# A linear-attention layer, an attention layer and two expert layers on one core: every item of a step placed by a table

## The reference

```python
x = x + 0.5 * ffn0(layernorm(x))        # int8-like weights CB, scale SCB, bias
x = x + deltanet(layernorm(x))          # the linear layer, below
x = x + 0.5 * ffn0(layernorm(x))
x = x + 0.5 * moe(layernorm(x))         # 16-head softmax attention, then 4 experts of 128-512-128
x = x + proj_ln_attn(layernorm(x))      # q, k, v each projected and layer-normed, one head
x = x + 0.5 * moe(layernorm(x))

def deltanet(x):                        # 8 heads of 16, J = 2 decays per head
    q, k = elu(x @ Wq.T) + 1, elu(x @ Wk.T) + 1
    v, beta, mix = x @ Wv.T, x @ Wbeta.T + bbeta, x @ Wmix.T + bmix
    gate = sigmoid(x @ Wgate.T + bgate)
    for t in range(256):                # carried state S (16x16) and z (16) per head and decay
        S = S * min(sigmoid(beta[t]) * r, 0.9999) + gate[t] * outer(k[t], v[t])
        z = z * min(sigmoid(beta[t]) * r, 0.9999) + gate[t] * k[t]
        y[t] = sum_j softmax(mix[t]) * (q[t] @ S) / (q[t] @ z + 1e-6)
    h = x + y @ Wout.T + bout
    return layernorm(h) * ln_g + ln_b
```

## Time and profile before

| | |
|---|---|
| median of 3 runs | 1615.6 us (1615.12 to 1621.57) |
| the profiled execution's own time | 1624.56 us |
| its span, first to last instruction | 1622.4 us |
| busy: PE, DVE, ACT, POOL | 74%, 58%, 51%, 42% |
| mean granted TensorE clock | 0.836 |
| largest wait in section 5 of the page | DVE's reduction L2075, 192.9 us idle before it |

### The profile page before, as it was taken

How to read it: one execution, slowest core, us unless ns; L and a number is a source line. 1 busy time by engine, 2 the same in 40 slices (tenths; PEclk the granted TensorE clock), 3 DMA queues, 4 the chain that set the end, 5 groups by cost and what they waited for, 6 DMA issues and landing times.

```text
span 1622.4 us, 30206 instructions
## 1 busy us (share of the span) xinstructions
PE 1193.1 (74%) x10624; PEld 774.4 (48%) x10624; DVE 942.2 (58%) x2992; ACT 822.2 (51%) x1849; POOL 688.0 (42%) x679
## 2 busy tenths in 40 slices
PE   3688888887446678988997567556667899899753
PEld 3566666655312335645555346333232565555543
DVE  5345556546336577677753696644667777775221
ACT  3444445443413557767775224232355777766532
POOL 4323333334622133555444566652213356544442
PEclk9878889888556789899999788866687999999977
DMA  7000000000022234443422120002223444442232
GB/s 240 1 2 1 1 2 2 1 1 2 2 78 80 80 98 135 129 143 117 125 76 77 45 63 24 12 1 78 80 80 98 139 133 147 133 134 73 64 106 71
DMA packets 116338, 116.71 MB, mean 72 GB/s; under 512 B 9288, under 2 KB 100040, under 8 KB 116040
## 3 DMA queue, kind: packets, MB, share of 16 engines
q1 hardware_dynamic: 105184, 77.99, 15.5%
q0 software_dynamic: 11008, 36.81, 7.0%
HBM read 73.01 MB, written 42.15 MB: 71 GB/s over the span
## 4 chain that ended last, share of the span: by engine, by line
PE 49%; DVE 14%; issue 8%; POOL 8%; ACT 8%; DMA 7%; SPq 5%; POOLq 0%; ACTq 0%; DVEq 0%
PE bank L1477 6%; PE bank L1514 6%; PE bank L1491 6%; PE bank L1535 5%; SPq L697 3%; DMA scr_m<-MH 2%; PE bank L1252 2%; DVE NM L2075 2%; PE bank L1310 2%; PE bank L1717 2%; PE bank L1553 2%; POOL scr_x L839 2%; POOL YG L847 1%; PE bank L1281 1%; SPq L662 1%
## 5 line engine op out<-in xcount | busy, mean ns | idle before, releaser
L2075 DVE TENSOR_REDUCE NM<-bank 128x2 f32<-128x512 f32 x512 | 338.0, 684 | 192.9 <-PE bank L1541 189.5
L1100 ACT ACTIVATE PBS<-bank 128x512 f32<-128x512 f32 x512 | 299.5, 600 | 219.5 <-PE bank L1535 216.1
L1535 PE MATMUL bank<-QS,KS 50*128 50x256 bf16 x1024 | 197.9, 295 | 100.2 <-DMA QS<-scr_m 49.4
L740 POOL TENSOR_TENSOR rs<-ve,half 128x4 f32<-128x4 f32 x88 | 89.9, 1022 | 421.2 <-DVE ve L1986 281.5
L1541 PE MATMUL bank<-KS,QS 48*128 48x256 bf16 x1024 | 208.5, 305 | 37.7 <-DMA KS<-scr_k 25.3
L1535 PEld LDWEIGHTS bank<-QS,KS 50*128 50x128 bf16 x1024 | 64.1, 97 | 231.5 <-issue 114.2
L1514 PE MATMUL bank<-PBS,V 128*32 128x256 f32 x2048 | 156.8, 429 | 1.4 <-ACT PBS L1100 1.4
L839 POOL DMA_INDIRECT scr_x<-XS,POS x64 | 63.8, 996 | 98.5 <-DVE POS L2041 83.9
L972 ACT ACTIVATE DB<-bank 128x512 f32<-128x512 f32 x64 | 38.5, 602 | 130.9 <-PE bank L1266 130.8
L1541 PEld LDWEIGHTS bank<-KS,QS 48*128 48x128 bf16 x1024 | 63.8, 98 | 66.4 <-DVE NM L2075 38.1
L1802 DVE TENSOR_TENSOR AB<-DB,bank 128x512 f32<-128x512 f32 x64 | 43.9, 685 | 81.7 <-ACT DB L972 47.7
(11 more groups left out here) (308 smaller groups left out, 2744.5 us busy)
## 6 DMA issues: line engine op xcount, KB each, us to landing
QS<-scr_q SPq DMA_DIRECT2D x64, 192.0 KB
KS<-scr_k SPq DMA_DIRECT2D x64, 192.0 KB
XD<-scr_x SPq DMA_DIRECT2D x16, 448.0 KB
scr_q<-PQ SPq DMA_DIRECT2D x32, 192.0 KB, 2.1
scr_k<-PQ SPq DMA_DIRECT2D x32, 192.0 KB, 2.2
scr_q<-PQ SPq DMA_DIRECT2D x32, 128.0 KB, 2.1
scr_k<-PQ SPq DMA_DIRECT2D x32, 128.0 KB, 2.1
scr_y<-YB SPq DMA_DIRECT2D x16, 256.0 KB, 2.3
```

Of the source, the lines that this page charges most:

```text
L740: pool.tensor_tensor(rs_[:, :], ve_[:, :], half[:, 0:ve_.shape[1]], ALU.pow).then_inc(rstd_sem, 1)
L1100: act.activation(PB[i % PB_SLOTS][:, :, :], bank[1 + i % 2][:, :].rearrange("p (k t) -> p k t", k=2), ACT.Exp).then_inc(A.e, 1)
L1535: last_s = pe.matmul(bank[1 + s % 2][:, k * T:(k + 1) * T], KS[1 - par][r, b, s // 2, k * P:(k + 1) * P], QS[1 - par][r, b, s // 2, :], st ...
L2075: dve.tensor_reduce(NM[:, 2 * b + qt, h:h + 3:2], bank[3 + i % 2][:, :].rearrange("p (u t) -> p u t", u=2), AX_X, ALU.max, negate=True).th ...
```

## The change

The linear layer's step becomes a loop over 16 slots, and a table LT gives every item of every engine its slot; ORDER is now sorted from it. AT, TAIL and ATTN have new numbers. LEADS is written with FFN_AT. No item is added, left out or changed in what it computes. One wait of POOL's YR asks for all earlier uses of bank 7 where it asked for those up to t1. The first part of the diff:

```diff
--- before.py
+++ after.py
@@ -46,24 +46,24 @@
 WROW = B2_AT + P
 
 
-AT = {"x_stats": 0, "x_moments": 0, "max1": 3, "div2": 6, "div3": 7, "z": 12, "z_stats": 13, "z_moments": 13, "q_mid":
-      11, "k_mid": 15, "acc": 14, "acc_stats": 17, "acc_moments": 17, "max0": 17, "take0": 24, "div0": 21, "div1": 24,
-      "x_add": 29, "take1": 30, "key": (21, 24, 25, 27, 28), "place": (30, 31, 31, 33), "m1T": 0, "turn2": 6, "turn3":
-      8, "x_turn": 7, "q": 9, "anT": 9, "k": 11, "wo": 12, "v": 13, "xd0": 14, "xd1": 14, "up": (15, 17, 19, 21, 23,
-      25, 27), "down": (18, 20, 21, 24, 27, 28, 30), "m0T": 17, "turn0": 19, "turn1": 24, "ranks": 30, "y": (4, 5),
-      "yt": 7, "qev": 9, "kev": 12, "anc": 9, "vev": 12, "zn": (17, 18), "en": (21, 22), "xt0": 13, "xt1": 14, "relu":
-      (15, 17, 19, 21, 23, 25, 27), "x_rstd": 0, "scatter": 2, "gather": 2, "v1": 4, "weights": 7, "rest1": (6, 14),
-      "z_rstd": 14, "rest2": (16, 17), "acc_rstd": 19, "xs": 20, "eg": 20, "yr": 28}
-
-
-TAIL = {"x_stats": 0, "x_moments": 0, "max1": 9, "div2": 6, "div3": 7, "z": 12, "z_stats": 13, "z_moments": 13, "q_mid":
-        13, "k_mid": 15, "acc": 11, "acc_stats": 16, "acc_moments": 19, "max0": 17, "take0": 24, "div0": 19, "div1": 24,
-        "x_add": 29, "take1": 30, "key": (21, 24, 25, 28, 28), "place": (30, 31, 31, 33), "m1T": 1, "turn2": 5, "turn3":
-        7, "x_turn": 7, "q": 6, "anT": 9, "k": 14, "wo": 12, "v": 13, "xd0": 14, "xd1": 15, "up": (15, 17, 19, 21, 23,
-        25, 27), "down": (18, 20, 21, 24, 27, 28, 30), "m0T": 18, "turn0": 21, "turn1": 24, "ranks": 30, "y": (4, 5),
-        "yt": 8, "qev": 9, "kev": 12, "anc": 9, "vev": 14, "zn": (17, 18), "en": (21, 22), "xt0": 13, "xt1": 15, "relu":
-        (15, 17, 19, 21, 23, 25, 27), "x_rstd": 4, "scatter": 0, "gather": 4, "v1": 4, "weights": 5, "rest1": (11, 14),
-        "z_rstd": 14, "rest2": (16, 17), "acc_rstd": 16, "xs": 20, "eg": 20, "yr": 29}
+AT = {"x_stats": 0, "x_moments": 0, "max1": 3, "div2": 6, "div3": 8, "z": 12, "z_stats": 13, "z_moments": 13, "q_mid":
+      12, "k_mid": 15, "acc": 15, "acc_stats": 17, "acc_moments": 17, "max0": 17, "take0": 23, "div0": 22, "div1": 28,
+      "x_add": 28, "take1": 30, "key": (21, 24, 26, 28, 28), "place": (31, 31, 31, 33), "m1T": 2, "turn2": 4, "turn3":
+      8, "x_turn": 7, "q": 9, "anT": 9, "k": 11, "wo": 12, "v": 13, "xd0": 14, "xd1": 15, "up": (15, 17, 19, 21, 23,
+      25, 27), "down": (18, 19, 21, 24, 27, 28, 30), "m0T": 16, "turn0": 19, "turn1": 24, "ranks": 30, "y": (4, 5),
+      "yt": 7, "qev": 9, "kev": 12, "anc": 9, "vev": 12, "zn": (17, 18), "en": (20, 23), "xt0": 13, "xt1": 15, "relu":
+      (15, 17, 19, 21, 23, 25, 27), "x_rstd": 0, "scatter": 3, "gather": 3, "v1": 4, "weights": 6, "rest1": (4, 14),
+      "z_rstd": 14, "rest2": (16, 16), "acc_rstd": 17, "xs": 17, "eg": 24, "yr": 29}
+
+
+TAIL = {"x_stats": 0, "x_moments": 0, "max1": 4, "div2": 5, "div3": 7, "z": 12, "z_stats": 12, "z_moments": 15, "q_mid":
+        12, "k_mid": 13, "acc": 13, "acc_stats": 16, "acc_moments": 17, "max0": 17, "take0": 27, "div0": 20, "div1": 29,
+        "x_add": 28, "take1": 30, "key": (17, 17, 20, 25, 25), "place": (31, 31, 31, 34), "m1T": 0, "turn2": 2, "turn3":
+        7, "x_turn": 9, "q": 9, "anT": 7, "k": 12, "wo": 15, "v": 9, "xd0": 15, "xd1": 15, "up": (15, 17, 19, 21, 23,
+        25, 27), "down": (18, 20, 21, 24, 27, 28, 30), "m0T": 15, "turn0": 20, "turn1": 23, "ranks": 30, "y": (5, 6),
+        "yt": 8, "qev": 3, "kev": 10, "anc": 10, "vev": 19, "zn": (17, 18), "en": (21, 23), "xt0": 14, "xt1": 15,
+        "relu": (15, 17, 19, 21, 23, 25, 27), "x_rstd": 1, "scatter": 2, "gather": 2, "v1": 0, "weights": 5, "rest1":
+        (11, 15), "z_rstd": 11, "rest2": (18, 22), "acc_rstd": 16, "xs": 24, "eg": 25, "yr": 30}
 
 
 def placed(slot):
@@ -73,30 +73,43 @@
 
 ATTN = {
     33: ((0, "pre"),),
-    39: ((0, "scale"), (0, "turn"), (0, "raw")),
+    39: ((0, "turn"), (0, "scale")),
+    41: ((0, "raw"),),
     44: ((1, "pre"),),
-    47: ((0, "norm"), (1, "scale"), (0, "yx"), (1, "turn"), (1, "raw"), (0, "kq")),
+    47: ((1, "scale"), (0, "norm"), (0, "yx"), (1, "turn"), (0, "kq"), (1, "raw")),
+    57: ((1, "yx"),),
     58: ((2, "pre"),),
-    61: ((2, "scale"), (1, "norm"), (1, "yx"), (0, "max"), (2, "turn"), (2, "raw"), (0, "exp"), (0, "main"), (3,
-        "pre")),
-    68: ((1, "kq"),),
+    60: ((2, "scale"),),
+    61: ((1, "norm"), (0, "max"), (2, "raw"), (2, "turn"), (0, "exp"), (0, "main"), (3, "pre")),
+    63: ((1, "kq"),),
+    68: ((2, "yx"),),
+    69: ((2, "norm"),),
     70: ((3, "scale"),),
-    71: ((2, "yx"), (2, "norm"), (1, "max"), (3, "turn"), (1, "exp"), (3, "raw"), (1, "main"), (2, "kq")),
-    76: ((4, "pre"),),
-    78: ((4, "scale"),),
+    71: ((1, "max"),),
+    72: ((1, "exp"),),
+    74: ((3, "turn"),),
+    75: ((3, "raw"), (1, "main")),
+    76: ((4, "pre"), (2, "kq")),
+    77: ((4, "scale"),),
     79: ((3, "norm"), (2, "max"), (4, "turn"), (2, "exp"), (4, "raw"), (2, "main")),
     80: ((3, "yx"),),
+    82: ((3, "kq"),),
     87: ((5, "pre"),),
-    90: ((5, "scale"), (3, "kq")),
-    93: ((4, "norm"), (3, "max"), (4, "yx"), (5, "turn"), (3, "exp"), (5, "raw"), (3, "main"), (5, "yx")),
+    89: ((5, "scale"),),
+    93: ((4, "yx"), (4, "norm"), (3, "max"), (5, "turn"), (5, "raw"), (3, "exp"), (5, "yx")),
+    102: ((3, "main"),),
     104: ((4, "kq"),),
-    106: ((6, "pre"),),
-    107: ((6, "scale"), (5, "norm"), (4, "max"), (6, "turn"), (4, "exp"), (6, "raw"), (4, "main"), (5, "kq")),
-    128: ((7, "pre"),),
-    130: ((7, "scale"), (6, "norm")),
-    131: ((6, "yx"), (5, "max"), (7, "turn"), (5, "exp"), (7, "raw"), (5, "main"), (6, "kq")),
-    132: ((7, "norm"), (6, "max"), (7, "yx"), (6, "exp"), (6, "main"), (7, "kq")),
-    133: ((7, "max"), (7, "exp"), (7, "main")),
+    105: ((6, "pre"),),
+    106: ((6, "scale"),),
+    107: ((5, "norm"), (4, "max"), (6, "turn"), (4, "exp"), (6, "raw"), (4, "main")),
+    109: ((5, "kq"),),
+    124: ((6, "yx"),),
+    125: ((7, "pre"),),
+    128: ((7, "scale"),),
+    130: ((6, "norm"),),
+    131: ((5, "max"), (7, "turn"), (5, "exp"), (7, "raw")),
+    132: ((5, "main"), (6, "kq"), (7, "norm"), (6, "max"), (6, "exp"), (6, "main")),
+    133: ((7, "kq"), (7, "max"), (7, "yx"), (7, "exp"), (7, "main")),
 }
 EXPERTS_AT = 133
 
@@ -115,12 +128,33 @@
 PACKED = _at
 
 
-ORDER = {1: (("yt", "pre"), ("mg", "pre"), ("cb0", "main"), ("q", "pre"), ("cb1", "main"), ("k", "pre"),
-             ("lw", "pre"), ("nst", "pre"), ("stk", "pre")),
-         6: (("t0", "post"), ("t2", "post"), ("v", "pre"), ("yo", "post"), ("s0", "main"), ("s2", "main"),
-             ("s4", "main")),
-         7: (("t1", "post"), ("t3", "post"), ("kt", "main"), ("wo", "post"), ("s1", "main"), ("s3", "main"),
-             ("s5", "main"))}
+FFN_AT = (0, 2, 4, 7, 8, 10, 12)
+LSLOTS = 16
+LT = {"weigh": (1, 3, 4, 6, 8, 10, 12, 13), "decay": (0, 2, 4, 6, 8, 10, 12, 13), "grow": (1, 2, 4, 6, 8, 10, 12, 14),
+      "yt": 0, "mg": 1, "cb": (4, 6), "scores1": 5, "nst": 11, "sums": (4, 7, 12, 1), "t": (2, 2, 4, 4), "kt": 9, "v":
+      7, "qk": (4, 6), "lw": 7, "yo": 8, "wo": 10, "s": (10, 12, 12, 14, 14, 15), "stk": 13, "scores0": 14, "a_yt": 0,
+      "a_ln": 4, "copy": (8, 1), "a_e1": 2, "a_cb": (3, 5), "a_qk": (4, 6), "a_kt": 9, "a_qx": 6, "a_we": 7, "a_yo":
+      8, "a_nst": 13, "a_stk": 13, "a_hn": 15, "a_x": 14, "vw": (0, 5), "qp": (1, 6), "yr": 4, "x_rstd": 6, "h_rstd":
+      12, "hg": 15, "d_mg": 1, "d_t": (3, 6), "d_sd": 3, "d_qf": 7, "d_lb": 3, "d_kf": 11, "d_gate": 6, "d_v": 8,
+      "x_stats": 7, "d_bt": 9, "x_moments": 10, "d_h": 12, "h_moments": 12, "d_s": (12, 12, 12, 14, 14, 14)}
+
+
+def order(b):
+
+    one = {1: (("yt", "pre"), ("mg", "pre"), ("cb0", "main"), ("cb1", "main"), ("nst", "pre"), ("q", "pre"), ("k", "pre"),
+               ("lw", "pre"), ("stk", "pre")),
+           6: (("t0", "post"), ("t2", "post"), ("v", "pre"), ("yo", "post"), ("s0", "main"), ("s2", "main"), ("s4", "main")),
+           7: (("t1", "post"), ("t3", "post"), ("kt", "main"), ("wo", "post"), ("s1", "main"), ("s3", "main"),
+               ("s5", "main"))}[b]
+
+    def slot(name):
+        if name in LT:
+            return LT[name]
+        return LT["qk"]["qk".index(name)] if name in "qk" else LT[name[:-1]][int(name[-1])]
+    return tuple(sorted(one, key=lambda use: slot(use[0])))
+
+
+ORDER = {b: order(b) for b in (1, 6, 7)}
 
 
 def uses(b, n, on, name=None):
```

In the loops each fixed number gives way to its entry of LT, as here on PE (the items stand in this order within a slot):

```diff
                                                  start=True, stop=True)
                         last.then_inc(L.full[1], 1)
 
-                    for i in range(8):
-                        if pre and i == 0:
+                    for i in range(LSLOTS):
+                        if pre and i == LT["yt"]:
                             pe.wait_ge(L.norm, n + 2)
                             turn(1, "yt", lambda t: Y0[other][:, t, :])
-                        if post and i == 0:
```

(52 more changed lines are left out.)

153 lines of the change are left out of this document (80 added, 73 removed).

## The result

The changed kernel takes **1527.63 us** (median of 4 runs, 1522.95 to 1530.24) against 1615.36 us before it on the same chip: a ratio of 0.9444 (95% interval 0.9411 to 0.9477), 88 us less. The forecast was 1585, with 1563 as the lower end. The sign was right and the size was not. The profiled execution took 1526.71 us (span 1524.9), 97.5 us less span than the profiled one before.

A forecast was written before the change was run, and what follows sets the result against it. No engine's total was taken to bound the kernel (PE busiest, 74%), so only PE's waits could go. Linear layer -23, AT -3 and tail -5 gave -31 us, 1615.6 to 1584.6, said as 1585; range 1576 to 1595, with neighbours 1563 to 1607.

The forecast's parts named there:

- The linear layer's order, 3.5 us a step of waits: Linear steps: reordering removes PE waits, walked as 3.9 us a step, taken as 3.5; -23 us in all.
- cb1's 1.2: Linear step: cb1's wait for q's two evacuations, 1.2 us, goes because scores1 now stands between.
- wo's 0.8: Linear step: wo's 1.9 us wait for yo's copy falls to about 1.1, gain 0.8.
- k's: Linear step: k's 1.7 us wait for cb1's copy shrinks as Ln and its loads run before q; gain 1.6.
- yo, which I had gain 0.6: Linear step: yo's 0.6 us wait for v's evacuation on DVE goes, since lw and d5 follow v.
- the states': Linear step: the states' 1.0 us wait for DVE's masking shrinks, gain 0.8.
- STK's: Linear step: new wait of d0' behind stk for ACT's copy, loss 0.6; a 0.5 us wait was to show.
- rival 2: Gains compound: linear steps' clock rises from 0.87 to 0.95, worth 1.9 us a step, giving 1572; chance 0.15.
- AT, -3: Expert layers' table: new order gains 3 us in all, from +5 to -12.
- m1T's wait of 1.0: Expert steps: m1T in slot 2 removes PE's 1.0 us wait for the last reduction, merely moved to slot 1's.
- The tail, -5 by scale(1): First expert tail: scale(1) before norm(0) avoids some 7 us of DVE contention with POOL; -5, from +8 to -12.
- The second tail, 0: Second expert layer's tail: z goes ahead of acc, but the chain keeps its order; 0 us, from +3 to -3.

The follow-up runs named there:

- scores1_back: Changed kernel with PE's scores1 alone put back behind k, ACT's Ln staying ahead of q's evacuation: 1528.53 us, ratio 0.9431.
- kt_back: Changed kernel with kt on PE put back ahead of v: 1533.70 us, ratio 0.9436.
- lin_alone: Changed kernel with the old AT, TAIL and ATTN, so only the linear layer's table is new: 1561.61 us, ratio 0.9623.
- norm_first: Changed kernel with norm(0) put back ahead of scale(1) on DVE, in ATTN: 1536.42 us, ratio 0.9492.
- tail_alone: Kernel before with only the new TAIL and ATTN: 1611.32 us, ratio 0.9938.
- at_alone: Kernel before with only the new AT: 1598.93 us, ratio 0.9884.
- fill_new: Changed kernel with the score matmuls of slot 2 issued six times over in every expert step: 1537.94 us, ratio 0.9474.
- fill_full: Changed kernel with the repeated score matmuls of slot 2 in expert steps 4 to 7 of each layer alone: 1532.35 us, ratio 0.9444.

## Why the prediction was right or wrong

- **The linear layer's order, 3.5 us a step of waits: nearly right in sum.** PE's idle time in the five full steps was 200.1 less 165.8 of busy time, 6.9 us a step, and is 2.9 now (160.8 less 146.5, over five). That is 4.0 gained, against a walk of 3.9. The sum came out partly by luck, as its terms show.
- **Its terms: wrong.** I added five waits as if each had its own worth. cb1's 1.2 and wo's 0.8 are worth 0.5 and 0.2 of idle time by themselves (scores1_back, kt_back), since yo's wait behind them takes up the rest; k's was worth 2.1 of idle time, not 1.6, and scores1 another 1.0 with Ln late. yo, which I had gain 0.6, lost 0.8. wo's wait fell by 1.5, not by 0.8, and the states' by 0.7 of the 0.8. The 0.5 us of new wait for Ln did not come, and STK's came with 0.5.
- **The step that failed first: the clock, put at nothing in the sum.** I priced the linear steps by idle time alone. The same matmuls of a step take 3.9 us less, from 33.2 to 29.3 us busy, as the clock goes from 0.87 to 0.98. That is as much again as the waits, and the direction of rival 2. It had a chance of 0.15 and a price of 1.9 us a step for 0.08 of clock. By its own slope, 2.8 us for 0.12, a rise of 0.11 gives 2.6; measured 3.9. With its price rival 2 would have said 1572, 44 us above the measured time.
- **Which steps count: wrong.** I gave 4.5 us to the steps up to the first X and 1 to the two behind the full ones. They gave 10 to 11, and 13.8 (34.5 and 36.2 us, now 24.4 and 32.5). Some 3 us of the 13.8 are matmuls that now lie ahead of the first X, so the gain ahead of it is larger by as much. Where the rest went was not tried.
- **AT, -3: wrong, it is about -19, give or take 10.** m1T's wait of 1.0 went, as said. Full steps idle 4.1 to 4.3 us, but for one, where lin_alone's idle 4.6 and the kernel before idles 4.5 to 5.5. Wrong was to price the order by idle time alone: PE's busy time fell by 1.5 us a step against the kernel before and by 3.0 against the step of lin_alone, as the half level got shorter. Why it got shorter stays open.
- **The tail, -5 by scale(1): near in number by luck, wrong in reason.** Profiles give -4.0 for this pair and about -9 over all kernels. The contention that the 5 us were reckoned from is worth 0, and its 8.54 us were misread as the length of two POOL products, which is 6.95. I had counted kq(0)'s later start, but took only 3.6 of the 8 us for it, where it took all.
- **The second tail, 0: within its range**, 184.0 and 181.9 us.
- **What was to show it.** The waits for CB and for re gone, STK at 0.5, scale(1) at 1.1: as said. The wait at L1296 gone: no, it grew to 1.3. The one at L1372 about 1: 0.4. Steps of 35 to 37 us: 32.2 on average. The wait at L1592 gone: yes, but the one for the reduction grew by 0.75 a step only against lin_alone (5.4 and 6.9 in two steps); against the kernel before it did not in the second layer (7.1). No 15 us before turn(1): 6.75.

The forecast fell 57 us short. Some 19 of them are the clock in the five full linear steps (3.9 each), some 19 the linear layer's steps around them (10 to 11 and 13.8, where 5.5 were said), which no run takes apart, some 16 AT and some 5 the tails. Rows 3 showed that steps with the same instructions differ by 2 us with the clock, and I kept that in a rival instead of the sum.

## What to carry to other kernels

Where steps with the same instructions show different granted clocks, a wait of PE can have two prices, its own length and the half level behind it: here 4.0 us less of idle time in a linear step went with 3.9 less of busy time. It is no fixed rate: Ln put back alone gave 1.2 us of busy time for 2.1 of idle, and scores1 or kt put back gave idle time and a higher clock. So give the clock a term and a range of its own. Waits of one step are not a sum: put one back alone, and see whether the next one shrinks, before you count it. An ACT table switch (Ln and Exp, 2 x 1.28 us) belongs where no copy that PE waits for stands behind it.

## What the runs showed of the hardware that was not expected

- Behind 3 us of gaps PE ran at the half level for 3.4 us in one order and 9.8 us in another, busy without a gap in both.
- The wait before yo was 1.4 to 1.5 us in four steps with the same instructions, and the half level followed it in two of them. scores1_back had 0.5 us more of idle time in a step and none of the half level.
- In the first ffn the views give a clock of 1.00, but its matmuls took 441 ns in one execution and 306 in another. Within one layer of norm_first their mean falls from 441 ns up to 41 us of the span to 287 behind it, and in tail_alone from 441 up to 37 us to 293. The traces' first clock records stand at just these times (at 63 us in the kernel before, at 26 in at_alone), so ahead of them the 1.00 is no reading. There the mean of one matmul tells the speed.
- 20 more matmuls in a step, with no wait removed, brought its clock from 0.96 to 1.00 and made it 1.1 us shorter on average in fill_new, and left it at 0.96 in the second layer of fill_full.
- A change from Exp to Ln and back cost ACT two loads of 1.28 us, and the next activation started 0.01 us behind each.
